# Second attention of a transformer kernel: router logits from the output product, one product for both batches' softmax sums, the constant row added by GpSimd

## The reference, cut to what matters

```python
x = x + first_attention_block(layernorm(x), ctx)      # with s4d and an MLP
x = x + first_moe(layernorm(x))                       # 8 experts, top 2
x = x + xattn(layernorm(x), ctx)                      # 16 heads of 8 channels
x = x + second_moe(layernorm(x))                      # 8 experts, top 2, LoRA

def xattn(q, kv):                                     # Wq bq Wk bk Wv bv Wo bo scale
    attn = softmax(heads(q @ Wq + bq) @ heads(kv @ Wk + bk).T * scale[0])
    return merge(attn @ heads(kv @ Wv + bv)) @ Wo + bo

def second_moe(x):
    scores = softmax(x @ Wg.T)                        # 128 -> 8 logits
    w, idx = top_k(scores, 2); w = w / w.sum()
    ...                                               # the two experts' MLPs, weighted
```

## Time and profile before

| | us |
|---|---|
| median of three executions | 960.75 |
| profiled execution, first to last instruction | 1025.8 |
| of it, combine_rows | about 557 to 594 |
| of it, second attention: opening and march | 594 to 800 |
| of it, tail with bias and table | 800 to 844 |
| TensorE busy / VectorE busy / ScalarE busy / GpSimd busy | 741.2 / 685.5 / 456.1 / 575.1 |

### The profile page before, as it was taken

The page is one execution under the profiler, slowest core; times in us unless marked ns, Lnnn a source line. Parts: engine busy times, 40 slices in busy tenths (PEclk is TensorE's granted clock), DMA queues, the critical chain, the costliest instruction groups (busy, mean ns, idle before and its releaser), DMA issues. The chain is left out here.

```text
span 1025.8 us, 21613 instructions
## 1 busy us (share of the span) xinstructions
PE 741.2 (72%) x6690; PEld 525.1 (51%) x6690; DVE 685.5 (67%) x3220; ACT 456.1 (44%) x1217; POOL 575.1 (56%) x944
## 2 busy tenths in 40 slices
PE   0687889796749999429892279989898756877750
PEld 0344445453736565225561157766666535777650
DVE  6998899887236876761110848977878564777754
ACT  3656665554004554202231747755556214544430
POOL 6788888868355442026663744455655452556550
PEclk9867887867559999768996559988988667999985
DMA  6300114994129785013542300000000016766517
GB/s 130 69 7 9 40 52 87 98 82 59 41 120 288 246 251 161 11 12 67 87 116 74 112 1 4 8 23 21 25 19 24 25 39 200 220 191 203 160 36 246
DMA packets 98690, 93.94 MB, mean 92 GB/s; under 512 B 37497, under 2 KB 82288, under 8 KB 98001
## 3 DMA queue, kind: packets, MB, share of 16 engines
q1 hardware_dynamic: 91126, 78.82, 31.1%
q0 software_dynamic: 6592, 13.58, 5.2%
q10 hardware_dynamic: 858, 0.17, 0.1%
HBM read 47.24 MB, written 43.19 MB: 88 GB/s over the span
## 5 line engine op out<-in xcount | busy, mean ns | idle before, releaser
L2342 POOL DMA_INDIRECT expert_pairs<-e_ys,e_home x78 | 78.9, 1011 | 76.5 <-DVE e_ys L2364 58.1
L1766 POOL DMA_INDIRECT expert_slots<-r_rows,r_slotu x64 | 63.2, 988 | 47.8 <-DVE r_rows L2095 31.7
L1750 POOL TENSOR_SCALAR a_kb<-a_kr,a_m,a_bk 128x128 f32<-128x128 f32 x128 | 57.5, 449 | 49.5 <-ACT a_kr L1963 32.9
L918 DVE MATCH_REPLACE8 work<-m,work 128x64 f32<-128x64 f32 x384 | 75.6, 205 | 0.0
L2309 PE MATMUL e_ps<-e_XH,e_wh 128*128 128x256 f32 x156 | 49.1, 315 | 26.7 <-DVE e_hh L2376 23.4
L1948 ACT ACTIVATE a_pp<-a_dd 128x512 f32<-128x512 f32 x64 | 40.2, 629 | 59.7 <-DVE a_dd L2135 57.2
L1537 POOL DMA_INDIRECT ex_rows<-rows,slot_source x32 | 30.7, 961 | 53.3 <-POOLq L1215 43.9
L905 DVE MAX8 m<-work 128x8 f32<-128x64 f32 x384 | 56.9, 207 | 0.0
L793 PE MATMUL psf<-filmw,us 97*128 97x512 f32 x64 | 51.3, 897 | 1.1 <-ACT FO L814 1.0
L2174 DVE RECIPROCAL a_rt<-a_pso 128x128 f32<-128x128 f32 x31 | 29.5, 953 | 30.7 <-PE a_pso L1876 21.3
L1591 ACT ACTIVATE ex_hs<-ex_psh,vec 128x512 f32<-128x512 f32 x32 | 20.9, 687 | 65.4 <-remote 36.2
(11 more groups left out here) (443 smaller groups left out, 2388.1 us busy)
## 6 DMA issues: line engine op xcount, KB each, us to landing
expert_slots<-rt_unfilled SPq DMA_DIRECT2D x151, 130.0 KB, 2.9
e_wf<-folded_weights SPq DMA_DIRECT2D x39, 386.0 KB
e_xr<-expert_slots SPq DMA_DIRECT2D x39, 130.0 KB
planes<-rt_zeros SPq DMA_DIRECT2D x4, 1024.0 KB
ew<-in_L_ffn_ew SPq DMA_DIRECT2D x16, 256.0 KB
comb_y<-planes SPq DMA_DIRECT2D x16, 256.0 KB, 5.7
pair_y<-expert_pairs SPq DMA_DIRECT2D x16, 256.0 KB, 5.8
folded_weights<-fold_done SPq DMA_DIRECT2D x8, 384.0 KB, 4.1
```

What stands on the lines that cost most here:

```text
L918: return own.did(dve.match_replace(wk_[x.j][:, h, :], m8[x.j][:, h, r, :], src[:, h, :], TAKEN))
L1750: m = pool.tensor_scalar(kb[a.j][:, :, h, :], k, m4[:, h:h + 1], bk4[:, h:h + 1], ALU.mult, ALU.add)
L1766: pool.indirect_dma_start(G.slots, bass.IndirectOffsetOnAxis(ap=slot[:, b, k, t:t + 1], axis=0), rb[b % NB][:, k, t, :], None).then_inc(se ...
L2342: pool.indirect_dma_start(G.pair, bass.IndirectOffsetOnAxis(ap=home[i % NY][:, k:k + 1], axis=0), ys[i % NY][:, k, :], None).then_inc(kept ...
```

## The change: what it does, and the diff

1. `G.X` becomes the first 128 columns of `G.XE` [128, 32, 136]. The eight extra columns hold the centred router logits of the row as far as they are known.
2. In combine_rows an opening builds `wgt = Wg.T`, `cols = colsum(wgt)`, and eight extra columns for Wo (`Wo @ wgt`) and for the constant row (`cst @ wgt`). After each block is normed and turned, TensorE multiplies the turned rows by `wgt`, and VectorE makes the row's own part of the logits from it (`base`): times the standard deviation, plus mean times `cols`. GpSimd gives the standard deviation (one instruction more per block).
3. In the attention the output product has 136 columns instead of 128, and so brings the logits with it. The turning of finished rows, their copy by ScalarE and the eight-column product go.
4. The constant row is no longer a product: GpSimd adds it (136 wide) to the row of tile x+1 in slot x, after `kb`.
5. The 16 products for the softmax sums, eight per batch with 64 columns, become eight with 128 columns.
6. `centre_logits` subtracts from SBUF instead of from PSUM; the tail loses the waits and steps of the row turning.

```diff
@@ combine_rows
-                        inverse_root(pool, step, ln[(b - 1) % 2], s["root"])
+                        step.then(pool.tensor_scalar(w["v"][:], w["mv"][:, :, 1], EPS, None, ALU.add))
+                        step.then(pool.tensor_tensor(w["rstd"][:], w["v"][:], w["half"][:, 0:TB], ALU.pow))
+                        after(pool, s["base"], b - 4)
+                        pool.tensor_tensor(std[(b - 1) % 4][:], w["v"][:], w["rstd"][:], ALU.mult).then_inc(s["root"], 1)
...
+                def base(q):
+                    w = ln[q % 4]
+                    dve.wait_ge(s["logits"], q + 1)
+                    step.did(dve.tensor_tensor(sl[:], psl[q % 2][:].rearrange("p (k e) -> p k e", e=NE), wide(std[q % 4][:].unsqueeze(2), shape), ALU.mult))
+                    step.then(dve.tensor_tensor(mc[:], wide(w["mv"][:, :, 0].unsqueeze(2), shape), wide(cols[:].unsqueeze(1), shape), ALU.mult))
+                    dve.tensor_tensor(G.XE[:, tiles(q), D:DE], sl[:], mc[:], ALU.add).then_inc(s["base"], 1)
+                    dve.wait_ge(s["base"], q + 1)
...
-                for b in range(NBLK + 1):
+                for b in range(NBLK + 4):
...
+                    if b >= 4:
+                        base(b - 4)
...
+                    if b > 1:
+                        q = b - 2
+                        pe.wait_ge(s["turned_sb"], q + 1)
+                        after(pe, s["base"], q - 1)
+                        for k in range(TB):
+                            t = q * TB + k
+                            mm = pe.matmul(psl[q % 2][:, k * NE:(k + 1) * NE], G.XF[:, t * P:(t + 1) * P], wgt[:], start=True, stop=True)
+                        mm.then_inc(s["logits"], 1)
@@ second_attention_and_router, GpSimd
+                def add_constant(g):
+                    row = G.XE[:, g.t, :]
+                    pool.tensor_tensor(row, row, cst[:], ALU.add).then_inc(s["based"], 1)
...
+                    if x.by(1).real():
+                        add_constant(x.by(1))
@@ TensorE
-                        if n.real():
-                            pe.wait_ge(s["x"], n.t + 1)
-                            mm = pe.transpose(psx[:, 384:512], G.X[:, n.t, :], G.ident[:])
...
-                    if l.real():
-                        logits(l)
...
-                    for b in range(2):
-                        for odd in range(2):
-                            for i in range(4):
-                                mm = pe.matmul(out[32 * i:32 * i + 32, 256 + T * b:256 + T * b + T],
-                                               ones[:, odd].rearrange("p s o d -> p (s o d)"),
-                                               pt[c.j][:, 2 * i + odd, T * b:T * b + T], start=odd == 0, stop=odd == 1)
+                    for odd in range(2):
+                        for i in range(4):
+                            mm = pe.matmul(out[32 * i:32 * i + 32, P:2 * P], ones[:, odd].rearrange("p s o d -> p (s o d)"),
+                                           pt[c.j][:, 2 * i + odd, :], start=odd == 0, stop=odd == 1)
...
-                    pe.matmul(out, G.onesrow[:], cst[0:1, :], start=True, stop=False)
-                    pe.matmul(out, of[d.j][:], wo[:], start=False, stop=True).then_inc(s["y"], 1)
+                    pe.matmul(out, of[d.j][:], wo[:], start=True, stop=True).then_inc(s["y"], 1)
@@ ScalarE
-                    if n.real():
-                        after(act, r["logits"], n.t - 1)
-                        act.activation(xf[n.j][:], psx[:, 384:512], ACT.Copy).then_inc(r["xf"], 1)
@@ VectorE
-                    dve.wait_ge(r["logits"], (b + 1) * TB)
-                    TT(w["lg"], psl.rearrange("p (k e) -> p k e", e=NE), w["mc"], ALU.subtract).then_inc(r["lg"], 1)
+                    dve.wait_ge(s["x"], (b + 1) * TB)
+                    TT(w["lg"], G.XE[:, tiles(b), D:DE], w["mc"], ALU.subtract).then_inc(r["lg"], 1)
...
-                    row = G.X[:, d.t, :]
+                    row = G.XE[:, d.t, :]
                     dve.wait_ge(s["y"], d.t + 1)
+                    dve.wait_ge(s["based"], d.t + 1)
                     TT(row, row, result(d.t), ALU.add).then_inc(s["x"], 1)
```

More of the change, by code:

```diff
@@ L1036, in combine_rows @@
         ln = [{n: C.sb(f"comb_{n}{j}", [P, TB] + k, ctx=ctx) for n, k in (("st", [6]), ("mv", [2]), ("v", []), ("rstd", []))} | {"half": G.half}
-              for j in range(2)]
+              for j in range(4)]
         pst = [C.ps(f"comb_pst{j}", [P, TB * P], ctx) for j in range(2)]
-        s = {n: C.sem("comb_" + n) for n in ("scaled", "pair", "sum", "var", "root", "xs", "turned", "turned_sb", "dve", "pool")}
+        std = [C.sb(f"comb_std{j}", [P, TB], ctx=ctx) for j in range(4)]
+        mc, sl = (C.sb("comb_" + n, [P, TB, NE], ctx=ctx) for n in ("mc", "sl"))
+        wot, cstt = (C.sb("comb_" + n, [P, P], ctx=ctx) for n in ("wot", "cstt"))
+        psc, psd = (C.ps("comb_" + n, [P, 512], ctx) for n in ("psc", "psd"))
+        psl = [C.ps(f"comb_psl{j}", [P, TB * NE], ctx) for j in range(2)]
+        wo, wg, wgt, cst, cols = G.att["wo"], *(G.moe[n] for n in ("wg", "wgt", "cst", "cols"))
+        bvi = VEC["L1_xattn_bv"][0]
+        s = {n: C.sem("comb_" + n) for n in ("scaled", "pair", "sum", "var", "root", "xs", "turned", "turned_sb", "dve", "pool",
+                                             "opened", "wgt", "rows_of", "cst", "cst_turned", "extra", "logits", "base")}
         fetched = [C.sem(f"comb_fetched{b}") for b in range(NBLK)]
@@ L1080, in _ @@
                         after(dve, s["turned"], q - 1)
-                        normalise_block(dve, xs[q % 2], G.X[:, tiles(q), :], ln[q % 2]).then_inc(s["xs"], 1)
+                        normalise_block(dve, xs[q % 2], G.X[:, tiles(q), :], ln[q % 4]).then_inc(s["xs"], 1)
             @block.tensor
             def _(pe):
[L1085 to L1090, removed]
+                pe.matmul(psd[:, 0:D], wide(G.vec[:, bvi:bvi + 1], [P, P]), wo[:, 0:D], start=True, stop=True).then_inc(s["rows_of"], 1)
@@ new lines, in _ @@
+                pe.transpose(psc[:, 128:128 + NE], wg[:], G.ident[0:NE, 0:NE])
+                pe.transpose(psc[:, 256:384], wo[:, 0:D], G.ident[:]).then_inc(s["opened"], 1)
+                pe.wait_ge(s["cst"], 1)
+                pe.transpose(psd[:, 0:P], cst[:, 0:D], G.ident[:]).then_inc(s["opened"], 1)
+                pe.wait_ge(s["cst_turned"], 1)
+                pe.matmul(psc[:, 0:NE], G.ones[:], wgt[:], start=True, stop=True)
+                pe.matmul(psc[:, 32:32 + NE], wot[:], wgt[:], start=True, stop=True)
@@ new lines, in _ @@
+                pe.matmul(psc[:, 64:64 + NE], cstt[:], wgt[:], start=True, stop=True).then_inc(s["opened"], 1)
+                for b in range(NBLK + 2):
+                    if b < NBLK:
+                        pe.wait_ge(s["xs"], b + 1)
+                        after(pe, s["turned_sb"], b - 1)
+                        for k in range(TB):
+                            mm = pe.transpose(pst[b % 2][:, k * P:(k + 1) * P], xs[b % 2][:, k, :], G.ident[:])
+                        mm.then_inc(s["turned"], 1)
+                    if b > 1:
+                        q = b - 2
+                        pe.wait_ge(s["turned_sb"], q + 1)
+                        after(pe, s["base"], q - 1)
+                        for k in range(TB):
+                            t = q * TB + k
+                            mm = pe.matmul(psl[q % 2][:, k * NE:(k + 1) * NE], G.XF[:, t * P:(t + 1) * P], wgt[:], start=True, stop=True)
+                        mm.then_inc(s["logits"], 1)
@@ L2233, in _ @@
                     dve.wait_ge(r["bias"], b + 1)
-                    rows = G.X[:, tiles(b), :].rearrange("p k d -> p (k d)")
-                    TT(rows, rows, pss[b // 2 % 2][:, b % 2, :], ALU.add).then_inc(r["bias_sum"], 1)
+                    rows = G.X[:, tiles(b), :]
+                    TT(rows, rows, pss[b // 2 % 2][:, b % 2, :].rearrange("p (k d) -> p k d", d=D), ALU.add).then_inc(r["bias_sum"], 1)
 def second_experts(nc, C, A, G):
```

105 lines of the change are left out of this document (39 added, 66 removed).

## The result

The changed kernel took 976.91 us in the median of five executions (970.59 to 977.45), the kernel before 960.75 (959.2 to 961.73): a ratio of 1.0143, interval [1.0104, 1.0182]. It is slower by some 14 us, where 958.1 was forecast. The traced execution of the changed kernel is the fastest of the five: its own time is 970.59 us, its span 969.4. Own time and span differ by 1.2 to 1.4 us in this and in each of the twelve traces that follow.

The account below looks back on a forecast made before the run. No engine was taken to bound the whole kernel, so the bound was sought stage by stage. Combine +5.6, first tiles -3.0, fours -3.75 and tail -1.5 gave -2.65, from 960.75 to 958.1 us; range 932 to 966.

Parts of the forecast that it names:

- the cost of the combine: combine_rows: `base` 2.6, later last root 0.3, end 2.3, opening 0.4; +5.6 us in all, 3.5 to 8.
- the end: combine_rows after the last copy to XF: four logit products 1.6 and one `base` 0.7 before the barrier, 2.3 us.
- the stalls: Attention: TensorE's products of ones held up while GpSimd issues scattering DMAs; 33 us, put down mainly to the profile.
- The forecast of 998 us for the profiled execution: Whole kernel under profile: 1025.8 us less 25 us of stall and 2.65 us of other gain.
- the stalls are real: Rival, attention: stalls happen without a profile too, so the median falls by 25 + 2.65 to 933 us; chance 0.30.
- First tiles: Attention up to tile 9: TensorE and ScalarE lose work, the two-tile loop shortens, 0.5 us per tile; -3.0 us.
- Fours: Groups of four march tiles, GpSimd setting the pace: 22.70 to 21.95 us, five times 0.75; -3.75 us (0 to -5).
- the rival that the clock falls: March: less TensorE work drops its clock, 2.1 us more per tile, five tiles +10.5, 968 us; chance 0.12.
- The rule I set aside: VectorE with two SBUF inputs contends with GpSimd reading SBUF; up to 0.5 us per add, 16 us, almost none expected.
- GpSimd's rival: Attention: adds not hidden, GpSimd becomes the bound, 23.0 us per four instead of 22.7; +4.9, 965.7 us; chance 0.15.
- Tail: Attention's end: VectorE's wait for logits goes, with two constants, turns and logits at half clock; -1.5 us (0 to -3).
- the ring: combine_rows, not forecast: VectorE's `base` waits for TensorE's logits, issued behind turns waiting for VectorE's norm; 11.55 us of waits.

Follow-up runs that it names:

- r9: The kernel before, unchanged, run in a third job to trace its stages without the long stalls: 966.47 us, ratio 1.0028.
- r2: combine_rows of the changed kernel with the attention of the kernel before: 1064.37 us, ratio 1.031 to the kernel before, in the job with stalls.
- r10: Changed kernel with `base` of block b-4 moved behind the norm, one set of statistics per block: 962.13 us, 0.9993 of the kernel before.
- r1: The kernel before, unchanged, profiled again in the job where it took 1032.91 us: 1036.1 us, ratio 1.0016.
- r3: Changed kernel without the rows' own part of the logits, so the changed attention alone: 1002.96 us, 0.9727 of the kernel before, job with stalls.
- r8: The kernel before with only the eight 128-column products of ones instead of sixteen of 64: 966.4 us, ratio 1.0051, job without stalls.
- r7: Changed kernel with all of `base` in one batch behind VectorE's last norm, TensorE's order left: 965.07 us, 1.0021 of the kernel before.
- r6: Changed kernel with logits of blocks 0 to 5 issued earlier, the other logits and all `base` in the attention's opening: 960.84 us, 0.996 of before.
- r11: r6 with GpSimd's constant added early, four tiles at once in slots -1 to 6: 956.83 us, 0.9983 of the kernel before.
- r4: Changed kernel with TensorE issuing the logits of block b-2 ahead of the turns of block b: 1014.75 us, 0.9867 of before, job with stalls.
- r12: r6 with the constant row as a product on TensorE again, none of it on GpSimd: 959.67 us, 0.9949 of the kernel before.

## Why the prediction was wrong

**The step that failed** is the cost of the combine: "Blocks 0 to 3 stand ahead of the statistics of blocks 4 to 7: 4 x 0.66 = 2.6", in a sum of **+5.6**, bounds 3.5 to 8. Measured is +18.7 (r9 against the changed kernel; r2 has the same 18.8 by itself). I had priced `base` by its instructions. I had named what stands behind it on VectorE, but not what it waits for: logits that TensorE issues behind turns, which wait for VectorE. The wait is 11.55 us in the trace, and one statement moved takes 11.2 us off combine_rows (r10).

**Its second half, the end**, was mis-sized: 2.3 us for one block's products and one `base`. Three blocks' products stand behind the last turns, 24 records in 5.12 us, and the end is +5.1. My 0.4 to 0.6 us for a product of two records was right (5.12 / 12 = 0.43); the count was wrong.

**Where the stalls belong.** I held that "the profile itself slows something by at least 65 us". It doesn't (r1): the traced and the untraced time of a kernel are one, and the stalls belong to a job. The forecast of 998 us for the profiled execution compared two sorts of job; 969.4 came, and 34 us of the fall from 1025.8 lie in the second experts (155.0 against 120.6), which the change doesn't touch. Nor does a run show the gap of about 6 us that the prediction gave for a profile's total: own times lie 1.2 to 1.4 us above the spans. That the change would clear away most of the stall is borne out where it occurs, 33.5 us of the attention (r3); which part of the change does it is open, since r8 met no stalls. The rival "the stalls are real" was right for a job like that; the one in which the forecast was measured was of the other sort.

**The attention** was forecast at -8.25 us in all and measured at -9.4. That the two lie near is luck: of the three terms one came as forecast, one by another way, one with the wrong sign.

**First tiles**: forecast -3.0, measured -3.1, the quiet tile 4.29 us against a forecast of 4.4 to 4.5. The idle time before the reciprocal (0.56 us in the earlier trace rows) is gone, in the changed kernel's timeline of a quiet tile:

```profile
637.26 0.28 DVE L2170 BATCH_NORM_STATS2 r_st<-X 128x6 f32<-128x128 f32 x1
637.46 0.94 DVE L2176 RECIPROCAL a_rt<-a_pso 128x128 f32<-128x128 f32 x1
```

**Fours**: forecast -3.75, measured -7.6 for tiles 9 to 30, by another way. An undisturbed four got longer, 23.08 to between 23.55 (r7) and 24.18 us, where I had 22.70 to 21.95. The gain comes from the two fours of 27.8 and 28.0 us with a fallen clock, fours that the changed kernel does not have. That less work for TensorE makes a fall of the clock cheap was no case of mine; I had only the rival that the clock falls. It does, to a mean of 0.72 to 0.93 in one to three tiles of each four, but not at the 2.1 us per tile of that rival: r7's fours take 23.55 us at 0.86 as at 1.00. How much of the -7.6 is left depends on how often the clock falls in the kernel before; r8 has 133.7 us for these tiles where r9 has 139.3.

**The rule I set aside.** I expected "almost none" of the contention between VectorE and GpSimd in SBUF. It is 0.77 us in each four (r6 and r11), most of what an undisturbed four lost, and up to 1.06 us on one instruction in r4. The reciprocal, which reads PSUM, keeps its 0.94 us beside an add; the small router operations read SBUF twice, and those I had left out. GpSimd's rival was right in sign for the fours, wrong in mechanism: VectorE was stretched, GpSimd did not run out of time (it still waits 1.5 us per four for VectorE's gates in the changed kernel).

**Tail**: forecast -1.5, measured +1.3. VectorE's wait for the logits is gone, but it led nowhere: GpSimd sets the end. From its first root in the tail to the end of the phase both kernels take 40.7 to 40.9 us (r9 and changed), the scattering DMAs following each other every 1.27 us. The 1.3 us lie ahead of that root. VectorE writes the march's last gates 2.7 us behind the tail's first scores in the changed kernel, 1.2 us behind them in r9 and in r11, where no add lies in the late slots. So it is most likely the adds of the march that leave VectorE behind; no run takes them out of the last slots alone.

With the ring and the end gone, little is left to gain: r6, r11 and r12 lie at 0.995 to 0.998 of the kernel before, with 1.0019 inside r11's interval. I forecast 0.997, but the attention's share of it came by another way than mine.

## What to carry to other kernels

When a step is added to an engine's order, follow its wait from engine to engine until it comes back to the same one: if the producer's instruction stands behind one that waits for this engine's last result, the step costs the whole loop per turn and not its own length, and moving it by one place in either engine's order (r4, r10) is the cure. Count what is still to be issued when the last block arrives, block by block. And small adds handed to an engine with free time are paid by its neighbour where both read SBUF; put them where the neighbour reads PSUM or idles.

## What the runs showed of the hardware

- The same kernel took 961 to 966 us in three jobs and 1033 in a fourth. Most of the difference is in stages where GpSimd issues scattering DMAs beside TensorE: second experts 150.8 against 120.5 us, attention 264.6 against 235.4. In the attention TensorE stands with gaps marked "issue", 11.0 us of them in r1's products of ones; in r1's second experts only 4.0 us are so marked, and 18.8 are waits for VectorE's `e_hh` that r9 doesn't have. The job with the stalls and the two later ones ran on three different chips, so job and chip can't be told apart, and what makes the difference I can't say.
- A VectorE operation of 0.16 to 0.18 us took 0.46 beside a GpSimd instruction of 0.47, and 1.24 beside one of 1.27: it ends with the other. A reciprocal of 0.94 that reads PSUM kept its length beside such an add (r6).
- In a four with 17 to 20 us of TensorE work of 23.55, a mean granted clock of 0.86 instead of 1.00 cost nothing (r7); in one with 20.7 of 23.08, a mean of 0.75 cost 4.75 us (r9).
- A product with 8 columns took 0.43 us at the lower clock level (24 records in 5.12 us), the turn of 128 columns 0.28 (4 in 1.11).
